# One block for scan, choice of experts and experts, with results added to the output by POOL

## The reference, cut to what matters

```
x = x + xattn(layernorm(x), fside, ctx) on the first stage's own weights (front part)
x = x + FFN of 1376 inner columns, weights looked up in a table of 16     (front part, then inside the scan)
x = x + scan(ctx, z = layernorm(x)):
        state = state * exp(dt * A) + (dt * u) * B ; y = <state, C> + D * u ; y * silu(z)
h = layernorm(x)                                  # 2048 rows
probs = softmax(h @ gate_w)                       # 32 experts
w, sel = top_k(probs, 8) ; w = w / sum(w)
for every expert e: rows sent to it (at most C = 1024, in the order of the rows)
        y_e = (silu(xg @ w_gate[e]) * (xg @ w_up[e])) @ w_down[e]          # 512 -> 192 -> 512
x = x + sum over the 8 chosen of w * y_e
```

## Time and profile before

| | |
|---|---|
| median of 3 runs | 2120.91 us (2116.69 to 2123.33) |
| profiled execution | 2115.85 us, its span 2114.1 us |
| mean granted clock of TensorE over the span | 0.853 |
| busy: PE, DVE, ACT, POOL | 1531.1, 1440.6, 905.1, 673.9 us |
| HBM over the span | 271.83 MB read, 181.40 MB written, 214 GB/s |

### The profile page before, as it was taken

One profiled execution on the slowest core, in us unless ns is written; L12 is line 12 of the kernel. 1 busy time (PEld: TensorE's weight loads), 2 busy tenths in 40 slices (PEclk: granted clock), 3 DMA queues, 4 the chain that ended last, 5 costly groups with the idle time before them and its releaser, 6 DMA issues. The chain is left out here.

```text
span 2114.1 us, 26326 instructions
## 1 busy us (share of the span) xinstructions
PE 1531.1 (72%) x9312; PEld 1303.2 (62%) x9312; DVE 1440.6 (68%) x2096; ACT 905.1 (43%) x1579; POOL 673.9 (32%) x450
## 2 busy tenths in 40 slices
PE   5767787774599699699689442105999999999920
PEld 3444454443499589589679431105888899998820
DVE  6676786864898999999999452003666655558954
ACT  3535555453444544534534140003555666665510
POOL 1010000101544644644554136770000000007876
PEclk9879788977699799799799775557999999999965
DMA  7888798844637338437435045653668666668877
GB/s 222 294 280 299 242 361 306 268 155 146 249 127 293 148 125 296 155 112 277 178 129 176 25 151 203 255 212 128 200 208 287 210 210 210 210 209 312 294 216 232
DMA packets 167496, 455.04 MB, mean 215 GB/s; under 512 B 17328, under 2 KB 19376, under 8 KB 157632
## 3 DMA queue, kind: packets, MB, share of 16 engines
q1 hardware_dynamic: 90880, 280.11, 39.6%
q10 hardware_dynamic: 56000, 106.06, 13.7%
q0 software_dynamic: 20480, 67.13, 9.2%
HBM read 271.83 MB, written 181.40 MB: 214 GB/s over the span
## 5 line engine op out<-in xcount | busy, mean ns | idle before, releaser
L1116 POOL TENSOR_TENSOR mix_st<-mix_Bb,mix_du 128x2048 f32<-128x2048 f32 x64 | 293.4, 4584 | 278.6 <-DVE mix_st L1401 266.5
L1393 DVE TENSOR_TENSOR_SCAN mix_st<-mix_dA,mix_st 128x512 f32<-128x512 f32 x256 | 311.6, 1217 | 42.9 <-POOL mix_st L1116 22.3
L1802 POOL DMA_INDIRECT moe_gat<-x_by_expert,moe_where x128 | 155.6, 1216 | 513.0 <-DMA x_by_expert<-moe_ys 471.1
L1266 ACT ACTIVATE mix_dA<-mix_dt,mix_A 128x512 f32<-128x512 f32 x256 | 177.0, 691 | 285.1 <-DVE mix_st L1393 281.4
L1187 PE MATMUL mix_G<-mix_xThi,mix_wup 128*128 128x256 f32 x1408 | 278.9, 292 | 14.3 <-issue 14.3
L1926 PE MATMUL moe_G<-moe_xhi,moe_whi 128*128 128x288 f32 x768 | 234.5, 305 | 14.0 <-issue 10.3
L1187 PEld LDWEIGHTS mix_G<-mix_xThi,mix_wup 128*128 128x128 f32 x1408 | 232.4, 198 | 17.2 <-issue 15.8
L1926 PE MATMUL moe_G<-moe_xhi,moe_wlo 128*128 128x288 f32 x768 | 228.6, 298 | 9.6 <-issue 9.6
L1926 PE MATMUL moe_G<-moe_xlo,moe_whi 128*128 128x288 f32 x768 | 228.8, 298 | 8.2 <-issue 8.2
L1213 PE MATMUL mix_Y<-mix_ident,mix_st 128*128 128x128 f32 x1024 | 150.3, 297 | 92.1 <-DVE mix_st L1401 92.1
L2275 DVE TENSOR_TENSOR moe_xlo<-moe_T,moe_xhi 128x512 fp32r<-128x512 f32 (+1 forms) x160 | 101.9, 637 | 156.0 <-issue 79.9
(11 more groups left out here) (235 smaller groups left out, 3231.0 us busy)
## 6 DMA issues: line engine op xcount, KB each, us to landing
x_by_expert<-front_zeros ACTq DMA_DIRECT2D x16, 4096.0 KB, 20.8
mix_wup<-w_halves SPq DMA_DIRECT2D x44, 1024.0 KB, 5.5
moe_raw<-in_ew SPq DMA_DIRECT2D x32, 1280.0 KB
moe_xt<-x_by_expert SPq DMA_DIRECT2D x128, 256.0 KB
x_by_expert<-moe_ys ACTq DMA_DIRECT2D x128, 256.0 KB
mix_wdn<-w_halves SPq DMA_DIRECT2D x44, 512.0 KB, 6.3
front_idx<-in_idx SPq DMA_DIRECT2D x44, 384.0 KB, 8.4
w_halves<-front_wst SPq DMA_DIRECT2D x44, 384.0 KB, 7.6
```

Source lines behind the costliest of these rows:

```text
L1116: nc.gpsimd.tensor_tensor(st[:, g % STBUF, :, :], Bb[:, q, :, :], du[:, k % 2, :].unsqueeze(1).to_broadcast([P, NG, S]), ALU.mult).then_in ...
L1266: nc.scalar.activation(dA[:, :], dt[:, k % 2, :], ACT.Exp, scale=A[:, c, m:m + 1]).then_inc(da_ready, 1)
L1393: nc.vector.tensor_tensor_scan(r, dA[:, :], r, 0.0, ALU.mult, ALU.add).then_inc(scanned, 1)
L1802: pool.indirect_dma_start(out=gat[:, q, :], out_offset=None, in_=s["XG"], in_offset=bass.IndirectOffsetOnAxis(ap=where[:, i, k:k + 1], axi ...
```

## The change

- The two later blocks become one, `mix_and_experts_block`; tensors of the two stages lie over each other in SBUF at offsets written by hand (`Place`), and both share the PSUM arrays G, Dp and YY.
- A row of XG has 560 numbers (`PITCH`): 512 of the row, the token's number, 32 weights (probability over the sum of the 8 chosen, for every expert), and padding. Rows that no token fills hold the number 65536, which is out of bounds for the output.
- x3 goes straight to `out`. For batches 0 to 2, inside the scan of the next batch: third moments on DVE (slot 9), scale and shift on POOL (slot 9), normalisation in place on ACT (slot 12), store of the normalised rows to DRAM on SP (slot 14), and, in the last slots, a load of them into XB. Logits are plain 32-bit matmuls without halves.
- The choice of batches 0 and 1 stands on DVE between the moments and the gated product of batch 3's tail; `z_by_tanh` of batch 3 moves from POOL to DVE.
- POOL's sends: batch 0 with k = 0 and 1, then `scale_and_shift(2, 3)`, then the other batches, k = 0 and 1, then k = 2 to 7.
- ACT scales each result by its rows' weights when it copies it (`scale=meta[...]`); SP loads number and weights of each expert's rows by two small DMAs. Experts 0 to 7 store results to XG as before. For experts 8 to 31 POOL adds each tile to `out` by an indirect DMA with `compute_op=ADD` (5 per expert). In periods 9 to 28 it also adds two tiles of the experts 0 to 7, which SP loads back (`late_of_period`), 40 in all. Since two adds may meet in a row of the output, adds of different experts wait for each other's landing.
- Gathers, accumulates, `combine_weights`, the reload of x3 into XB and the final stores are gone.

The core of the diff:

```diff
+            inputs_product(0)
...
+            scale_and_shift(1, NB - 1)
+            pool.wait_ge(ids_made, 2)
+            pool.wait_ge(filled, 16 * (FILLS + 1))
+            sends(0, 0)
+            sends(0, 1)
+            scale_and_shift(2, NB - 1)
+            for k in range(2):
+                for b in range(1, NB):
+                    sends(b, k)
+            for k in range(2, TOP):
+                for b in range(NB):
+                    sends(b, k)
+            pool.wait_ge(x3_out, 16 * NB)
+            done = 0
+            for e in range(DEFER, E_N):    
+                pool.wait_ge(meta_in[e % MBUF], 32 * (e // MBUF) + 32)
+                if e > DEFER:
+                    all_out(pool, NT * e)
+                if done > 0:
+                    pool.wait_ge(late_added, 16 * done)
+                for j in range(NT):
+                    add_result(e, j)
+                for i in late_of_period(e):
+                    add_late(i, e)
+                    done = i + 1
...
+            def add_result(e, j):
+                n = NT * e + j
+                rows = TILE_ROWS[j]
+                pool.wait_ge(ys_ready, n + 1)
+                pool.indirect_dma_start(out=out_rows,
+                                        out_offset=bass.IndirectOffsetOnAxis(ap=meta[0:rows, e % MBUF, j, 0:1].bitcast(U32), axis=0),
+                                        in_=ys[0:rows, n % YBUF, :], in_offset=None, bounds_check=NB * S - 1,
+                                        oob_is_err=False, compute_op=ALU.add).then_inc(y_added[n % YBUF], 16)
+
+            def add_late(i, e):
+                q = i % LATE
+                rows = TILE_ROWS[i % NT]
+                all_out(pool, NT * e + NT)
+                if i > 0:
+                    pool.wait_ge(late_added, 16 * i)
+                pool.wait_ge(late_in[q], 32 * (i // LATE) + 32)
...
+            def result(e, j):
...
+                if n >= YBUF:
+                    before = n - YBUF
+                    if before < LATE_TILES:
+                        act.wait_ge(y_stored[n % YBUF], 16 * (before // YBUF) + 16)
+                    else:
+                        act.wait_ge(y_added[n % YBUF], 16 * ((before - LATE_TILES) // YBUF) + 16)
...
+                nc.scalar.activation(ys[0:rows, n % YBUF, :], YY[0:rows, n % 2, :], ACT.Copy,
+                                     scale=meta[0:rows, e % MBUF, j, 1 + e:2 + e]).then_inc(ys_ready, 1)
...
+            dve.wait_ge(made, 4)
+            shift(0)
+            choose(0)
+            shift(1)
+            for t in range(TT):
+                z_by_tanh(NB - 1, t)
+            place(0)
+            row_weights(0)
+            choose(1)
+            for t in range(TT):
+                gated(NB - 1, t)
+            for t in range(TT):
+                second_residual(NB - 1, t)
+            dve.wait_ge(x3_ready, NB)
+            moments(2, x2, range(TT))
+            aggregate(2)
+            place(1)
+            row_weights(1)
+            shift(2)
+            choose(2)
+            place(2)
+            row_weights(2)
+            shift(3)
+            choose(3)
+            place(3)
+            row_weights(3)
```

More of the change, by code:

```diff
@@ L882, with __init__, __call__ @@
 HN = NG // 2
+E_N = 32
+F = 192
+F2 = F - P
+TOP = 8
+TILES = NB * TT
+CAP = 2 * (NB * S * TOP // E_N)
+STRIDE = CAP + 4
+XROWS = E_N * STRIDE
+FILL = 16
+FILLS = XROWS // P // FILL
+GUC = 3 * P
+EW = DC * GUC
+RW = EW + 2 * D
+UNIT = 576
+HALF_U = UNIT // 2
+NT = -(-UNIT // P)
+TILE_ROWS = [min(P, UNIT - P * j) for j in range(NT)]
+OVER_T = 4
+OVER_R = (CAP - UNIT) // OVER_T
+RING = 7
+YBUF = 4
+LATE = 4
+MBUF = 4
+DEFER = 8
+META = 1 + E_N
+LATE_PER = 2
+AWAY = float(2 * XROWS)
+FIRST_BYTE = 16512
+LAST_BYTE = 229344
+class Place:
+    def __init__(self, nc, prefix, first, end):
+        self.nc, self.prefix, self.at, self.end = nc, prefix, first, end
+    def __call__(self, name, shape, dt):
+        size = math.prod(shape[1:]) * (2 if dt == BF16 else 4)
+        h = self.nc.alloc_sbuf_tensor_at(self.prefix + name, shape, dt, offset=self.at)
+        self.at += -(-size // 32) * 32
+        assert self.at <= self.end, (name, self.at, self.end)
+        return h
 def halves_of_slot(g):
@@ L900, in downs_of_slot, with mix_and_experts_block @@
     return early + halves_of_slot(g - 2)
-def mix_block(nc, d, s):
+def mix_and_experts_block(nc, d, s, out, filled):
     ALL = NB * UNITS
@@ new lines, in mix_and_experts_block @@
+        gw = sb("gw", [P, DC, E_N], F32)
+        mx = sb("mx", [P, TILES], F32)
+        pr = sb("pr", [P, TILES, E_N], F32)
+        top = sb("top", [P, TILES, TOP], F32)
+        rest = sb("rest", [P, TILES, E_N], F32)
+        mask = sb("mask", [P, TILES, E_N], BF16)
+        counted = sb("before", [P, TILES + 1, E_N], BF16)
+        key = sb("key", [P, TILES, E_N], F32)
+        near = sb("near", [P, TILES, TOP], F32)
+        where = sb("where", [P, TILES, TOP], U32)
+        total = sb("total", [P, TILES], F32)
@@ new lines, in send, with sends @@
+            def send(i, k):
+                pool.indirect_dma_start(out=s["XG"], out_offset=bass.IndirectOffsetOnAxis(ap=where[:, i, k:k + 1], axis=0),
+                                        in_=XB[:, i, :], in_offset=None, bounds_check=XROWS - 1,
+                                        oob_is_err=False).then_inc(sent[k], 16)
+            def sends(b, k):
+                if b < NB - 1:
+                    pool.wait_ge(xb_in[b], 16)
+                else:
+                    pool.wait_ge(norm_ready[2], TT * NB)
+                pool.wait_ge(where_ready, b + 1)
+                pool.wait_ge(meta_ready, b + 1)
+                for i in range(b * TT, (b + 1) * TT):
+                    send(i, k)
@@ new lines, in logits @@
+            def logits(b, t):
+                if b + t == 0:
+                    pe.wait_ge(g_in, 16)
+                    pe.wait_ge(scanned, NG * ALL)
+                if b == 1 and t == 0:
+                    pe.wait_ge(y_copied, NB * DC)
+                if b > 1 and t == 0:
+                    pe.wait_ge(rank_read, b - 1)
+                pe.wait_ge(rT_copied, TT * b + t + 1)
+                for c in range(DC):
+                    last = nc.tensor.matmul(YY[:, b % 2, t * E_N:(t + 1) * E_N], rT[:, b % 2, c, t * P:(t + 1) * P], gw[:, c, :],
+                                            start=(c == 0), stop=(c == DC - 1))
+                if t == TT - 1:
+                    last.then_inc(logits_ready, 1)
```

1566 lines of the change are left out of this document (702 added, 864 removed).

## The result

The changed kernel takes 2144.7 us (median of 4, 2138.1 to 2146.6) against 2120.5 for the kernel before (4 runs); the ratio is 1.011 with a 95% interval of 1.009 to 1.013. It is slower by 1.1%, where 2069 and a gain were forecast. The profiled execution has a span of 2143.6 us.

The account below looks back on a forecast made before the run. It saw three stretches without matmuls, some 340 us, as what there is to win. 2114.1 + 10 - 40 - 15 - 78 + 76 = 2067, with 1.75 around the span 2069; range of 8 in 10, 1970 to 2250.

Parts of the forecast that it names:

- part 4: POOL's adds of result tiles to the output in DRAM: waits on landings lengthen periods 9 to 28, +76 us.
- A cycle is thus four times (issue + landing L): Expert periods 9 to 28: four adds wait in a row for ys slots, 21.4 us per period against 17.6.
- L = 3.6: Landing time in us of one POOL add to the output; 2.67 or less costs nothing, 6.4 costs 300 us.
- The issue is that of the gathers beside VectorE's work, mean 1.27: POOL's issue of one add: 1.27 plus 0.30 us; undisturbed 1.28 would lower the sum by 23 us.
- Part 2: Choice of experts and POOL's sends: sends resume at 1250 after batch 3's choice and end at 1393 against 1433.6, -40 us.
- part 1: Scan: third moments and normalisations of batches 0 to 2 move into it, +10 us, between 0 and +18.
- Parts 3 and 5: Experts: periods of 17.6 us, -15, and final 83 us become 5, -78; fills with 9% more bytes, 0.
- Case B: Slower: POOL's adds land as late as gathers, deciding from 4.2 us; 2293 us at 6.4, chance 0.22.
- A: Rival: POOL's adds fit, landing under 2.7 us, no stall in the experts' periods; 1993 us, chance 0.17.
- C: Rival: each POOL add stops PE for 1.7 us, periods of 29.6 us; slower, 2267 us, chance 0.10.
- D: Rival: sends no longer hold PE, experts 0 to 7 run beside them; 128 us less, 1941, chance 0.08.
- E: Rival: the choice of experts doesn't move, so its 40 us gain stays out; 2109 us, chance 0.05.

## Why the prediction was wrong

**The direction failed by part 4, the price of a wait on POOL.** The chain of adds cost 525.0 - 20 x 17.6 = 173 us instead of 76. The step that failed is "A cycle is thus four times (issue + landing L)": it has no term for the time from a landing to POOL's next issue, beyond the 0.30 us that also stand between two issues without a wait, and it takes the issue from the wrong instruction. Measured, POOL's next issue begins 0.94 to 1 us behind the landing, three times per period. The term that I said the forecast hangs on, **L = 3.6**, was nearly right: the three landings are 2.84, 4.48 and 3.76, mean 3.7, under the 4.2 that I had named as the point where the change turns slower. The send's row couldn't show the missing term, since there SP waited, and SP's load began 0.05 us behind the landing. That the mean came out near 3.6 is in part luck: it is a mixture of adds that land after about 3 and of those beside the weights' load, and no row had either.

**The issue was too short.** "The issue is that of the gathers beside VectorE's work, mean 1.27": an add's is 1.54. I put the difference between 0.97 and 1.27 down to VectorE, by the Trainium skill ("DMA: Bandwidth & Descriptors", section "SWDGE vs HWDGE vs iDMA": VectorE's two-port mode locks POOL out of the memory in which it writes descriptors), and wrote that the trace agrees. For gathers it does: the eight with VectorE idle took 1.01. For adds it doesn't: in the changed kernel they take 1.54 beside VectorE's work and with VectorE idle alike. For plain writes it does in part: in the run where every write waits, the ten with VectorE idle took 0.97 at most, and of the 160 there are 33 of 1.07 to 2.16 us, all beside one operation of VectorE (L2260, the low halves of the activations), while 117 others beside its work, that operation included, took no more than 1.05. Whether the lock is the reason, no run here shows. So most of the 1.54 is what adding costs, and no saving of 23 us lay there.

**The formula had the wrong members and nearly the right sum.** "ys has 4 slots ... so result (e+1, 4) waits until add (e+1, 0) has landed": ACT does wait there (202.7 us in the waits view), and yet five slots don't shorten the period. POOL issues four more adds meanwhile, 7.4 us, longer than the landing of the first and the result behind it. The cycle is seven issues and three landings. With my values that is 7 x 1.57 + 3 x 3.6 = 21.8 in place of 21.4. The wait that the formula was built on was real, and it was not what set the period.

**The chain, term by term**, per period: 0.4 for the formula, 7 x 0.27 = 1.9 for the issues, 3 x 0.69 = 2.1 for the time behind the landings over the 0.30, 3 x 0.09 = 0.3 for the landings, 0.2 for the first period's wait for ACT. Together that is 4.9, against the measured 26.25 - 21.4, and 97 us in 20 periods. The issues cost 38 us of it and the time behind the landings 41. Either one alone would still have left a gain by the forecast's sum; the landings are 5.

**Part 2 held, and its effect was larger.** The sends end at 1404.9 instead of 1433.6, -29 with part 1 where -30 was forecast, though the scan had started 10 us late. Batch 3's sends wait for its places and weights until 1254.8 (forecast 1250). The first result follows 13.3 us after the last send's end, where the kernel before needed 25.4: 12 us more than forecast. Part 1 was 7.0 instead of 10.

**The block's start was missed**, 9 us. I had counted the boundary that goes, not the clears that move with it; these are some 6 of the 9.

**Parts 3 and 5 held.** In the version without late tiles nearly every period is 17.6 and the span 1975.8, where the sum without part 4 was 1991; the fills' 9% and all else in the front cost 1.6.

**The account**, on the spans: forecast 2067, plus 97 for the chain (173 - 76), minus 11 for the first result (1418.2 instead of 1429), minus 10 for the last experts, for which TensorE had worked ahead during the stall (12.5 and 13.0 us from one expert's first add to the next one's, in place of 17.6), is 2143; measured 2143.6.

**The rivals.** Case B has the right outcome (slower, periods of 25 to 33 with ACT waiting), but not for its reason: the landing's mean is 3.7, not above 4.2. No rival had the time behind the landing. A falls: no landing with late tiles was under 2.7 in the mean. C falls: TensorE is full beside five adds a period. D, which I had at 0.08, did not come with the change: where TensorE isn't held, the experts run beside the sends in the kernel before too. E falls: the first send begins at 1217.9.

## What to carry to other kernels

When a queue waits for its own landings in a row, write down its cycle as issues, landings, and the time from each landing to the next issue (0.94 us on POOL here), and take each from an engine and an operation like it: a row in which another engine waits hides the last of the three. What decides is how many landings stand in series, since five adds per period without such waits cost nothing here. Before deferring work to get past a busy engine, ask when that engine is free again: the deferral of experts 0 to 7 covered sends that were already over, and cost 166 us. Merging blocks moves their set-up to the front too; sharing it among four engines gave back some 6 us.

## What was unexpected

- An indirect add takes 1.54 us to issue, whether VectorE works or not, against 0.97 for most indirect writes with the same rows.
- POOL issues again 0.30 us behind an issue without a wait, but 0.94 us behind a landing that it waited for; SP began a load 0.02 us behind the same landing.
- A scattered write of 256 KB lands 1.8 us after its issue's end beside the sends, and about half of those beside the experts' work do too, but after 4.7 beside the loads of the weights and the next tiles; an add after 3.1, and 4.5 to 5.2 beside those loads.
- The same program took 2119 us on three chips and 2006 on two others, all by TensorE's pace under the sends. On the first kind one matmul begins per 2.8 us.
- Under the stall the granted clock was 0.84 in place of 1.00, a mix of the two levels; the matmuls of the gate and up weights took 328 ns in the mean of the whole run instead of 305, in a stage that waited for POOL anyway.
